# Node degrees in a two-layer graph network: a full histogram over all edges, and a count of run maxima with one gathered run per node

## The reference, cut to what matters

```python
def gcn_conv(x, edge_index, W, b):          # called twice, hidden 64, out 128
    n = x.shape[0]
    h = x @ W
    ...                                     # loops are added to src, dst
    deg = jax.ops.segment_sum(ones, dst, num_segments=n)
    dinv = jnp.where(deg > 0, jax.lax.rsqrt(deg), 0.0)
    norm = dinv[src] * dinv[dst]
    msg = h[src] * norm[:, None]
    out = jax.ops.segment_sum(msg, dst, num_segments=n)
    return out + b

h = jnp.maximum(_layernorm(x, axis=-1), 0.0)
x = x + _L0_gnn_ref(h, edge_index, ...)     # gcn_conv, relu, gcn_conv
h = jnp.maximum(_layernorm(x, axis=-1), 0.0)
x = x + _L1_gnn_ref(h, edge_attr_64, ...)   # w = mlp(edge_attr); m = w * (h[src] @ Wlin)
                                            # agg = segment_sum(m, dst); out = mlp(agg)
```

## Time and profile before

| | us |
|---|---|
| median of 3 runs | 3453.82 (3452.84 to 3453.93) |
| the profiled execution | 3451.63 |
| its span, from first to last instruction | 3449.9 |
| the degrees beside the first linear layer | 67 to 229 |
| from the degrees to the first adjacency product | 229 to 252 |
| first convolution with its adjacency blocks | 252 to 1,250, about |
| second convolution and first node layer | to 1,520, about |
| edge layer and last products | 1,520 to 3,450 |

### The profile page before, as it was taken

One profiled execution on the slowest core, in us unless ns is written; L12 is line 12 of the kernel. 1 busy time (PEld: TensorE's weight loads), 2 busy tenths in 40 slices (PEclk: granted clock), 3 DMA queues, 4 the chain that ended last, 5 costly groups with the idle time before them and its releaser, 6 DMA issues.

```text
span 3449.9 us, 82941 instructions
## 1 busy us (share of the span) xinstructions
PE 2932.2 (85%) x19882; PEld 2141.2 (62%) x19883; DVE 2095.0 (61%) x4806; ACT 946.5 (27%) x2058; POOL 1445.4 (42%) x1549
## 2 busy tenths in 40 slices
PE   6979999999999969978787878787788787778887
PEld 4742356777777759965555555555556565555555
DVE  7999999999999954344444444444444444444344
ACT  5110133455566621122121222222212121222221
POOL 0000000000000000037777777777777777777774
PEclk7989999999999989988887888888878888888888
DMA  2000011122222259943333333323333333333332
GB/s 63 0 0 0 39 57 76 76 94 104 104 113 113 113 201 352 347 137 79 82 82 82 82 82 82 82 80 85 80 81 82 82 82 82 82 82 82 82 79 70
DMA packets 289446, 325.50 MB, mean 94 GB/s; under 512 B 236303, under 2 KB 249640, under 8 KB 276606
## 3 DMA queue, kind: packets, MB, share of 16 engines
q1 hardware_dynamic: 234382, 218.90, 19.2%
q0 software_dynamic: 49504, 102.66, 10.4%
q10 hardware_dynamic: 5264, 1.36, 0.2%
HBM read 237.69 MB, written 85.09 MB: 94 GB/s over the span
## 4 chain that ended last, share of the span: by engine, by line
POOL 40%; PE 36%; issue 17%; DVE 5%; DVEq 1%; POOLq 1%; DMA 0%; ACT 0%; ACTq 0%; SPq 0%
POOL shared L544 40%; PE pb L1407 9%; PE pa L1407 9%; PE pc L1401 6%; PE pd L1401 5%; PE pd L1365 3%; PE pf L1367 1%; PE pb L1492 1%; DVE shared L1042 1%; DVE loop L1042 1%; DVEq L1042 0%; PE pa L1485 0%; PE pb L1619 0%; PE pb L1375 0%; PE pb L1566 0%
## 5 line engine op out<-in xcount | busy, mean ns | idle before, releaser
L544 POOL DMA_INDIRECT shared<-lin_table,idx x1516 | 1430.5, 944 | 463.8 <-issue 461.0
L1220 DVE TENSOR_TENSOR shared<-pb,shared 128x512 f32<-128x512 f32 x345 | 224.6, 687 | 1098.4 <-DMA shared<-lin_table,idx 1097.0
L573 POOL DMA_DIRECT2D lin_table<-c x12 | 9.2, 770 | 1497.6 <-issue 1308.5
L1566 PE MATMUL pb<-we_sb,shared 128*128 128x128 f32 x3136 | 609.9, 354 | 2.4 <-ACT shared L793 2.3
L1566 PEld LDWEIGHTS pb<-we_sb,shared 128*128 128x128 f32 x3136 | 517.3, 250 | 122.0 <-issue 115.9
L1562 PE MATMUL pb<-be_parts,ones 3*128 3x512 bf16 x392 | 178.1, 454 | 375.7 <-DVE shared L1220 375.3
L1042 DVE TENSOR_SCALAR shared<-col_h,shared 128x784 bf16<-128x784 f16 x1092 | 403.4, 418 | 5.1 <-issue 4.4
L666 ACT ACTIVATE idx<-idx_all 128x8 int32 (+1 forms) x196 | 40.5, 208 | 1134.8 <-issue 1131.5
L793 ACT ACTIVATE shared<-pa,be_col 128x512 f32<-128x512 f32 x392 | 247.8, 683 | 364.8 <-PE pa L1555 317.5
L1562 PEld LDWEIGHTS pb<-be_parts,ones 3*128 3x128 bf16 x392 | 36.5, 93 | 438.1 <-issue 419.5
L1407 PE MATMUL pb<-shared,c 128*128 128x392 bf16 x1568 | 304.0, 329 | 1.6 <-DVE shared L1042 0.9
(11 more groups left out here) (238 smaller groups left out, 3999.5 us busy)
## 6 DMA issues: line engine op xcount, KB each, us to landing
adjacency<-shared SPq DMA_DIRECT2D x49, 1568.0 KB, 5.6
shared<-adjacency SPq DMA_DIRECT2D x49, 1568.0 KB, 8.8
table_sb<-lin_table SPq DMA_DIRECT2D x3384, 0.5 KB
shared<-in_edge_attr_dram SPq DMA_DIRECT2D x195, 256.0 KB
table_sb<-lin_table ACTq DMA_DIRECT2D x2632, 0.5 KB
shared<-lin_table,idx POOLq DMA_INDIRECT x1516
lin_table<-c POOLq DMA_DIRECT2D x12, 256.0 KB, 7.2
out_dram<-xr SPq DMA_DIRECT2D x12, 256.0 KB
```

Of the source, the lines that this page charges most:

```text
L544: pool.indirect_dma_start(out=dest(s, j), out_offset=None, in_=table, in_offset=bass.IndirectOffsetOnAxis(ap=idx[:, s, j:j + 1], axis=0)). ...
L1220: dve.tensor_tensor(msgs[s % 2][:, h, :, :], pb[:, h, :].rearrange("p (i f) -> p i f", f=F), rows[:, h, :, :], ALU.mult).then_inc(msg_read ...
L1566: last = pe.matmul(pb[:, h, i * F:(i + 1) * F], act_t[:, h, i * P:(i + 1) * P], we2_sb[:, :], start=False, stop=(i == 3))
```

## The change

The histogram over all edges leaves the path that these inputs take, and stands only in the general path (`over` not zero). In its place:

- VectorE takes the maximum of each run of 64 edges (`half_max`, 32 runs a partition, 3,125 runs in all) and derives the unit maxima from them. One-hot tiles are made for the run maxima alone (4 ring slots instead of 196 groups), and TensorE multiplies them into a 64x98 histogram.
- Three small steps of TensorE, each copied out by VectorE, turn this into prefix sums: for each node, how many runs end below it. This is `half_at`, the number of the run in which the node's edges begin. They stand between the transposes of the sources.
- GpSimd gathers this run from `dst` in memory, for all nodes: 49 indirect DMAs of 128 rows of 64 numbers. VectorE compares the gathered numbers with the node's own, adds up those that are smaller, and adds 64 for each run below: `edges_below`. TensorE forms the difference to the next node, which is the degree.
- VectorE tests that `dst` is sorted (`falls`), inside rows and from row to row. A fall gives a count of 512 (`UNSORTED`) in one more column of `counts`, which leads to the general path.
- The first linear layer's turns have nothing between their transposes and products.

`every_other` is a view of the identity, `above` a triangle of ones, `to_next` a band of -1 and 1. The diff, cut to its core (left out: tile and constant declarations, GpSimd's constants, and the general path's copy of the histogram):

```diff
@@ -539,6 +567,26 @@
...
+            of_halves = dst.rearrange("(n e) -> n e", e=HALF)
+            pool.wait_ge(count_out, 4)
+            for b in range(NB):
+                pool.indirect_dma_start(
+                    out=half_rows[:, b, :], out_offset=None, in_=of_halves,
+                    in_offset=bass.IndirectOffsetOnAxis(ap=half_at[:, b:b + 1], axis=0)).then_inc(half_in, 16)
+
@@ -647,10 +695,9 @@
                 act.activation(tmsg[:, bass.ds(c * CB, CB), :],
                                pb[:, 0, 0:CB * HID].rearrange("p (b q) -> p b q", q=HID), ACT.Copy).then_inc(ln1.out, 1)
 
-            act.wait_ge(deg_ready, 1)
-            act.activation(count_sb[:, LOW:2 * LOW], count_ps, ACT.Copy).then_inc(count_out, 1)
-            act.wait_ge(deg_turned, 1)
-            act.activation(deg_sb[:, :], deg_ps, ACT.Sqrt, bias=1.0).then_inc(deg_ready, 1)
+            act.wait_ge(deg_turned, 2)
+            step(act.activation(deg_sb[:, :], first_deg_ps, ACT.Relu))
+            act.activation(deg_sb[:, :], deg_sb[:, :], ACT.Sqrt, bias=1.0).then_inc(deg_ready, 1)
 
@@ -873,15 +922,24 @@
 
             dve.wait_ge(raw_loaded, 16 * 8)
             dve.tensor_copy(raw_f[:, :, :], raw_d[:, :, :]).then_inc(raw_fp, 1)
-            by_unit = raw_d.rearrange("p k (q e) -> p (k q) e", q=U)
+            by_half = raw_d.rearrange("p k (q e) -> p (k q) e", q=HQ)
+            for m, op in enumerate((ALU.max, ALU.min)):
+                step(dve.tensor_reduce((half_max if op is ALU.max else half_tmp)[:, :], by_half, AX.X, op))
             for m, op in enumerate((ALU.min, ALU.max)):
-                step(dve.tensor_reduce(um_i[:, m, :], by_unit, AX.X, op))
+                halves_of = half_max if op is ALU.max else half_tmp
+                step(dve.tensor_reduce(um_i[:, m, :], halves_of.rearrange("p (n t) -> p n t", t=2), AX.X, op))
                 step(dve.tensor_reduce(mm_i[:, m * HALVES:(m + 1) * HALVES],
                                        um_i[:, m, :].rearrange("p (k q) -> p k q", q=U), AX.X, op))
             step(dve.tensor_scalar(um_i[:, :, :], um_i[:, :, :], 4, None, ALU.arith_shift_right))
             dve.tensor_copy(um_f[:, :, :], um_i[:, :, :]).then_inc(um_ready, 1)
             step(dve.tensor_copy(mm_f[:, :], mm_i[:, :]))
             dve.tensor_scalar(mm_f[:, HALVES:2 * HALVES], mm_f[:, HALVES:2 * HALVES], 1.0, None, ALU.add).then_inc(mm_ready, 1)
+            for keys_of, by, op in ((dlo, LOW - 1, ALU.bitwise_and), (dhi, 6, ALU.arith_shift_right)):
+                step(dve.tensor_scalar(half_tmp, half_max, by, None, op))
+                step(dve.tensor_copy(keys_of[:, 0:RING * U], half_tmp))
+            for s in range(RING):
+                for hot, keys_of, n in ((hist_lo, dlo, LOW), (hist_hi, dhi, HIGH)):
+                    dve.tensor_tensor(hot[s], numbers(n), pairs_of(keys_of, s, n), ALU.is_equal).then_inc(hist_hot, 1)
             dve.wait_ge(row_ready, 1)
@@ -894,14 +952,21 @@
...
             for m in range(4):
                 turned_copy(m, m, dst_f[:, :])
-            for m in range(4):
+            dve.wait_ge(hist_used, 1)
+            dve.tensor_copy(by_low, by_low_ps).then_inc(count_out, 1)
+            for m in range(2):
                 turned_copy(4 + m, m, idx_all[:, :])
+            dve.wait_ge(hist_used, 2)
+            dve.tensor_copy(high_sums, high_sums_ps).then_inc(count_out, 1)
+            for m in range(2, 4):
+                turned_copy(4 + m, m, idx_all[:, :])
+            dve.wait_ge(hist_used, 3)
+            dve.wait_ge(pool_consts, N_POOL + N_MORE)
+            dve.tensor_copy(count_sb[:, LOW:2 * LOW], halves_below_ps).then_inc(count_out, 1)
             dve.wait_ge(turned_out, 8)
-            step(dve.tensor_copy(dst_i, dst_f[:, :]))
-            step(dve.tensor_scalar(tmp_i, dst_i, LOW - 1, None, ALU.bitwise_and))
-            step(dve.tensor_copy(dlo, tmp_i))
-            step(dve.tensor_scalar(tmp_i, dst_i, 6, None, ALU.arith_shift_right))
-            step(dve.tensor_copy(dhi, tmp_i))
+            dve.wait_ge(deg_turned, 1)
+            step(dve.tensor_scalar(deg_sb[:, :], half_at_ps, float(HUNITS - 1), None, ALU.min))
+            dve.tensor_copy(half_at, deg_sb[:, :]).then_inc(count_out, 1)
             step(dve.tensor_scalar(tmp_i, idx_all[:, :], P - 1, None, ALU.bitwise_and))
@@ -961,15 +1026,25 @@
                 dve.tensor_copy(be2_parts[:, i, :], be2_res[:, :]).then_inc(consts, 1)
 
 
-            with dve.Fori(0, ITERS) as it:
-                for s in range(RING):
-                    g = it * RING + s
-
-                    dve.wait_ge(hist_used, it * RING + (s + 1))
-                    for hot, keys_of, n in ((hist_lo, dlo, LOW), (hist_hi, dhi, HIGH)):
-                        dve.tensor_tensor(hot[s], numbers(n), pairs_of(keys_of, g, n), ALU.is_equal)\
-                           .then_inc(hist_hot, 1)
-            dve.wait_ge(deg_ready, 2)
+            for k in range(HALVES):
+                step(dve.tensor_tensor(order_junk, raw_d[:, k, 0:GE - 1], raw_d[:, k, 1:GE], ALU.is_gt))
+                step(dve.tensor_reduce(falls[:, k:k + 1], order_junk, AX.X, ALU.max))
+            of_groups = bounds[:, :].rearrange("a (g m) -> a m g", m=2)
+            between = order_junk[0:1, 0:HALVES * P - 1]
+            step(dve.tensor_tensor(between, of_groups[:, 0, 1:HALVES * P], of_groups[:, 1, 0:HALVES * P - 1], ALU.subtract))
+            step(dve.tensor_reduce(row_falls[:, 0:1], between, AX.X, ALU.min))
+            step(dve.tensor_scalar(row_falls[:, 1:2], row_falls[:, 0:1], -1.0, None, ALU.is_lt))
+            step(dve.tensor_tensor(falls[0:1, 0:1], falls[0:1, 0:1], row_falls[:, 1:2], ALU.max))
+            step(dve.tensor_tensor(falls[:, 0:1], falls[:, 0:1], falls[:, 1:2], ALU.max))
+            step(dve.tensor_scalar(counts[:, NW:NW + 1], falls[:, 0:1], float(UNSORTED), None, ALU.mult))
+            step(dve.tensor_copy(node_ids[:, :], node_ids[:, :].bitcast(int32)))
+            step(dve.memset(edges_below[:, NB:NB + 1], float(N_EDGES)))
+            dve.wait_ge(half_in, 16 * NB)
+            step(dve.tensor_tensor(half_less, half_rows, bc(node_ids[:, :], HALF), ALU.is_lt))
+            step(dve.tensor_reduce(edges_below[:, 0:NB], half_less, AX.X, ALU.add))
+            dve.scalar_tensor_tensor(edges_below[:, 0:NB], deg_sb[:, :], float(HALF), edges_below[:, 0:NB],
+                                     ALU.mult, ALU.add).then_inc(count_out, 1)
+            dve.wait_ge(deg_ready, 1)
             step(dve.reciprocal(dinv[:, :], deg_sb[:, :]))
...
@@ -1300,6 +1402,9 @@
...
                             pe.wait_ge(turned_out, n + 1)
+                        if n == 2 and a == 1:
+                            pe.wait_ge(count_out, 1)
...
@@ -1309,9 +1414,28 @@
...
-
+                    for s in range(RING):
+                        pe.wait_ge(hist_hot, 2 * s + 2)
+                        for u in range(U):
+                            last = pe.matmul(by_low_ps, hist_lo[s][:, u // T, :, u % T], hist_hi[s][:, u // T, :, u % T],
+                                             start=(s == 0 and u == 0), stop=(s == RING - 1 and u == U - 1))
+                    last.then_inc(hist_used, 1)
+                    pe.wait_ge(pool_consts, N_POOL + N_MORE)
...
+            def to_blocks(to):
+                pe.matmul(to, count_sb[:, LOW:3 * LOW], every_other[:, 0, :], start=True, stop=False)
+                pe.matmul(to, count_sb[:, 0:2 * LOW], every_other[:, 1, :], start=False, stop=True).then_inc(deg_turned, 1)
+
+            pe.wait_ge(count_out, 2)
+            pe.matmul(halves_below_ps, by_low, above[0:LOW, 0:LOW], start=True, stop=False)
+            pe.matmul(halves_below_ps, above[0:HIGH, 0:HIGH], high_sums, start=False, stop=True).then_inc(hist_used, 1)
+            pe.wait_ge(count_out, 3)
+            to_blocks(half_at_ps)
 
             pe.wait_ge(um_ready, 1)
+            pe.wait_ge(count_out, 4)
             pe.wait_ge(turned_out, 8)
             pe.wait_ge(bounds_ready, 1)
@@ -1350,36 +1474,16 @@
...
-            def histogram(first, n):
-                with pe.Fori(0, n) as i:
-                    for s in range(RING):
-                        pe.wait_ge(hist_hot, (first + i) * (2 * RING) + (2 * s + 2))
-                        for u in range(U):
-                            last = pe.matmul(count_ps, hist_hi[s][:, u // T, :, u % T], hist_lo[s][:, u // T, :, u % T], start=False, stop=False)
-                        last.then_inc(hist_used, 1)
-                        pe.matmul(pf[:, :], zeros_b[:, :], wide, start=True, stop=True)
-
             with pe.Fori(0, CHUNKS) as c:
                 turn(ln1, c, lambda j: hch[:, j, :], P)
-                histogram(c * HIST, HIST // 2)
                 pe.wait_ge(ln1.ht, c + 1)
 
                 for j in range(CB):
                     last = pe.matmul(pb[:, 0, j * HID:(j + 1) * HID], cht[:, j, :], w1_sb[:, :], start=True, stop=True)
                 last.then_inc(ln1.mm, 1)
```

(8 more changed lines are left out.)

99 lines of the change are left out of this document (88 added, 11 removed).

## The result

The changed kernel takes **3393.36 us** (median of 3 runs, 3391.82 to 3394.16) where the one before took 3453.82: a ratio of 0.9827, 95% interval 0.9813 to 0.9841. It is faster by 60.5 us. The forecast was 3347.5, a gain of 106, and its range ended at 3363: the sign was right, the size was not.

A forecast was written before the change was run, and what follows sets the result against it. VectorE's histogram and the serial tail behind it were taken as the bound. Moving the reciprocal from 228.57 to 122.3 takes off 106.3 us: 3451.63 becomes 3345.3, plus 2.2 for the median, 3347.5 us; range 3334 to 3363.

The forecast's parts named there:

- What bounds the kernel: From 67 to 229 us, VectorE's histogram comparisons set the pace at 0.813 us a group; the first linear layer waits.
- The front: VectorE's work ahead of the turns: 2.2 + 3.25 + 0.6 - 5.06 = +1.0 us, first turn at 65.9.
- The turns: First linear layer's seven turns, a serial chain: 8.51 us each at the low clock, last product's copy at 120.7.
- The degrees: Layout products and two ScalarE activations behind the last turn: reciprocal at 122.3 instead of 228.57, 106.3 us less.
- the landing: Arrival of the gathered rows after the last gather: taken as 2 us, bounds 0 and 7.2.
- The hidden work: GpSimd's gathers, 33 to 94.4, then VectorE's counts at 103.8, covered by the turns with 12 to 17 us slack.
- The step that failed: The stage's end moves everything behind it one to one, so the 106.3 us gained there reach the kernel's end.
- that tail: Serial work behind the histogram: layout, root, reciprocal at 228.57, scaling and splitting; TensorE does nothing until 251.
- The clock stays high: Rival: TensorE keeps its full clock through the turns, reciprocal at 109.2, kernel at 3334.4 us; chance 0.12.
- The gathers are late: Rival: VectorE's work holds up GpSimd's gathers by 32 us, reciprocal at 137.5, kernel at 3362.7 us; chance 0.11.
- The general path: Rival: the order test finds a false fall, both convolutions gather, kernel near 7,000 us; chance 0.01.

The follow-up runs named there:

- a_warm: The kernel after, with unused products (3 and 8 of 512 columns a turn) filling TensorE's gaps in the first linear layer's turns: 3379.82 us.
- b_plus24: The kernel before, with 23 more semaphore increments that nobody waits for in VectorE's stream ahead of its adjacency loop: 3498.51 us, ratio 1.0139 to before.
- a_plus71: The kernel after, with 70 more instructions (semaphore increments) in VectorE's stream ahead of its wait for the gathers, loop at 649 to 1367: 3346.93 us.

## Why the prediction was right in its front and wrong in its sum

**What bounds the kernel.** Right: with the histogram gone the turns became the serial chain, and the layout products waited for them alone (121.70; counts since 109.82).

**The front.** +1.0 us was forecast, the first turn at 65.9; it came at 64.34, 0.6 ahead of before. This error of 1.6 us and the next one have opposite signs, and by this luck the reciprocal was met within 1.2.

**The turns.** 8.51 us each with the clock at the lower of its levels (1.2 of 2.4 GHz) from the second on; measured 8.86, clock 0.50. The first turn's transposes ran at 1.00, and the clock fell at 67.16, in the middle of its products. The fall in the front was the right row to go by. The last copy came at 122.05 (forecast 120.7), 57.7 us behind the first turn's start where 54.8 were forecast. The rule in the Trainium skill (TensorE: Matmul & The Clock Gate, "Why this matters for your kernels") did not hold here: the clock fell behind gaps of 1.05 and 1.01 us.

**The degrees.** Reciprocal at 123.46 (forecast 122.3), a gain of 105.1 us (106.3). Its comparison and sum took 3.43 and 3.42 us (3.6 and 3.5), the landing 102.69 - 101.13 = 1.56 (2).

**The hidden work.** Gathers end 101.13 (94.4), since two of them were long beside the scans and four more somewhat long; counts 109.82 (103.8). Of a slack of 12 to 17 us 11.7 were left, so it cost nothing.

**The step that failed** is "All later stages start from that tail, and none of their work can begin earlier. So the stage's end sets everything behind it one to one". It holds for the start of the next stage (105.4 us won at its first product) and not for its length, which the prediction took as fixed: "stages behind 251 change their length, for which I see no reason". There was a reason. Its two halves could be read beforehand, a loop of 719 instructions whose fetches are seen in q14, and 24 instructions more ahead of it; its price could not, since no row of the kernel before has such a gap. A term was missing, the loop's place: 49.5 us, 2.06 an iteration on average. With it the sum of the prediction is 3347.5 + 49.5 = 3397, against the 3393.36 measured. Most of the rest is in the medians: by the two profiled executions the gain is 57.5 us (3451.63 to 3394.16), by the medians 60.5.

**The rivals.** *The clock stays high*: not so, but a_warm made it so by force, with the reciprocal at 113.51 (the rival's sum said 109.2, without the unused products and with counts in time). *The gathers are late*: 6.7 us late, with 11.7 left. *The general path*: not taken.

**What is shown and what stays open.** Shown: the loss lies in the adjacency loop, it comes and goes with the place of VectorE's loop in its stream alone, in both kernels and in both directions; each slow kernel has one packet of instructions an iteration more; and VectorE's long gaps stand at the jump back to the loop's first instruction and end 1.76 to 1.96 us behind a packet's start in all 23 jumps of the kernel after. Open: why the packet with the loop's head starts behind the branch when the loop touches seven blocks, and 1.5 us and more ahead of it when it touches six. Both kinds execute the same hint at the loop's head, and no run was made without it. How the loss would be with another loop length wasn't tried either.

## What to carry to other kernels

Where an engine fetches a loop's instructions anew in each iteration, as VectorE does here, the loop's place in the stream can be a cost of its own: any edit ahead of it, even one that only removes work, can add or take a fetch in each iteration. Read the instruction queue's packets before and after, and divide the difference by the count of iterations; if it comes out whole, move the loop by a few dozen instructions and measure again before judging the edit. When single iterations are compared, take the same ones in both kernels, cut at the same instruction. And when work is cut from the front, check the length of every later stage as well as its start.

## What the runs showed of the hardware that I had not expected

- One block more of VectorE's instructions in each of 24 iterations costs 49.5 us (b_plus24: 50.4), 2.1 us an iteration, with 24 x 8.2 KB in q14. TensorE's loop of 730 instructions, moved by 204 places, showed nothing of the kind.
- What costs is the jump back: 2.06 us from the branch to the loop's first instruction instead of 0.55, since the packet starts behind the branch. VectorE goes on 1.76 to 1.96 us behind the packet's start.
- The Trainium skill (Runtime: NRT & Kernel Launch, "Instruction fetch mechanics") says that instructions come in blocks of 256, that the cost of crossing into the next is mostly hidden, and that a branch out of what is held makes a stall. The last agrees with these runs: the long gaps stand at the jump. The second agrees where the loop touches six blocks: before, VectorE's gaps are 3.9 us in the whole stage. The first doesn't: a_plus71, six and seven packets an iteration and the size of a packet speak for 128.
- More instructions can be faster: 70 increments more made the kernel after 46 us faster.
- Unused products in TensorE's gaps, 11 a turn, brought the granted clock from 0.50 to 1.00 and gained 9.95 us up to the reciprocal.
